# The value products of two cross attentions: f32 operands replaced by pairs of f16 halves

## The reference, cut to what matters

```python
# layer 1, x and ctx of width 256
Q, K, V = (q @ W_q.T), (ctx @ W_k.T), (ctx @ W_v.T)          # in 16 heads
scores = where(mask, einsum('bhqd,bhkd->bhqk', Q, K) / sqrt(16), -1e10)
x = x + (softmax(scores) @ V).reshape(B, 64, 256) @ W_proj.T + b_proj
# layer 3: q and k normalised to length 1, q times exp(scale), a bias instead of a mask
q, k = l2norm(x @ Wq + bq) * exp(min(scale_mul_log, log(100))), l2norm(ctx @ Wk)
x = x + (softmax(einsum('bhqd,bhkd->bhqk', q, k) + attn_bias) @ (ctx @ Wv)) @ Wo + bo
```

## Time and profile before

| | |
|---|---|
| median of 3 runs | 2602.82 us |
| the profiled execution | 2618.47 us, span 2616.8 us |
| mean granted TensorE clock | 0.959 |
| TensorE busy | 2341.9 us, 89% |
| VectorE, ScalarE, GpSimd busy | 64%, 48%, 32% |
| loop of layer 1, first to last value product | 409.3 to 785.6 us |
| loop of layer 3, first to last value product | 1949.7 to 2375.9 us |

### The profile page before, as it was taken

One profiled execution on the slowest core, in us unless ns is written; L12 is line 12 of the kernel. 1 busy time (PEld: TensorE's weight loads), 2 busy tenths in 40 slices (PEclk: granted clock), 3 DMA queues, 4 the chain that ended last, 5 costly groups with the idle time before them and its releaser, 6 DMA issues. The chain is left out here.

```text
span 2616.8 us, 44501 instructions
## 1 busy us (share of the span) xinstructions
PE 2341.9 (89%) x17350; PEld 1491.5 (57%) x17397; DVE 1665.0 (64%) x3199; ACT 1245.8 (48%) x2066; POOL 826.7 (32%) x669
## 2 busy tenths in 40 slices
PE   6866779999997879999999999699889999998898
PEld 4744446666673445566556666356546666666554
DVE  4986455545537666888888864644665565654577
ACT  2326234444454214555555554566445555554465
POOL 5610042224203421323333210045544444433153
PEclk8988899999998989999999999899989999999999
DMA  3200453322214016677767664033322222220132
GB/s 112 69 1 1 137 135 93 99 76 69 77 32 163 1 60 143 115 142 147 149 122 138 122 118 79 33 103 103 98 64 78 69 74 74 64 63 21 62 92 63
DMA packets 358467, 226.44 MB, mean 87 GB/s; under 512 B 289785, under 2 KB 326483, under 8 KB 358259
## 3 DMA queue, kind: packets, MB, share of 16 engines
q1 hardware_dynamic: 355186, 215.20, 34.0%
q0 software_dynamic: 3072, 8.39, 1.1%
HBM read 114.87 MB, written 0.52 MB: 44 GB/s over the span
## 5 line engine op out<-in xcount | busy, mean ns | idle before, releaser
L100 PE MATMUL PS<-hot 128*128 128x512 f16 x459 | 143.9, 456 | 90.0 <-DVE l0a_g L1087 17.5
L3875 POOL TENSOR_TENSOR l2x_rows<-l2x_rows,l2x_one 128x256 f16<-128x256 f32 (+2 forms) x95 | 100.2, 1081 | 379.5 <-DVE l2x_rows L1441 379.5
L3981 PE MATMUL PS<-l2x_rows,l2x_pth 128*128 128x512 f16 x832 | 200.3, 379 | 1.6 <-DVE l2x_mean L4178 1.6
L3625 DVE CUSTOM_DVE_ANT_0 l1x_junk<-PS,l1x_bias 128x1024 bf16<-128x1024 f32 (+1 forms) x128 | 123.2, 992 | 96.1 <-PE PS L3286 95.2
L3625 DVE CUSTOM_DVE_ANT_0 l3x_junk<-PS,l3x_bias 128x1024 bf16<-128x1024 f32 (+1 forms) x128 | 123.8, 991 | 46.6 <-PE PS L3286 45.5
L4171 DVE TENSOR_TENSOR l2x_pl<-l2x_sc,l2x_ph 128x1664 f16<-128x1664 f32 x64 | 123.8, 1934 | 39.8 <-ACT l2x_ph L4051 37.8
L4156 DVE CUSTOM_DVE_ANT_0 l2x_sc<-PS,l2x_bias 128x1665 f32<-128x1665 f32 x64 | 120.9, 1889 | 41.8 <-issue 40.6
L4069 ACT ACTIVATE l2x_meanT<-PS 128x256 f32<-128x256 f32 x64 | 24.6, 384 | 247.7 <-PE PS L3943 247.7
L3496 ACT ACTIVATE l3x_pT<-PS 128x512 f32<-128x512 f32 x144 | 84.6, 594 | 120.2 <-PE PS L3332 117.8
L100 PEld LDWEIGHTS PS<-hot 128*128 128x128 f16 x459 | 47.3, 112 | 165.7 <-issue 47.7
L3935 PE MATMUL PS<-l2x_kh,l2x_qth 128*128 128x512 f16 (+1 forms) x512 | 132.8, 341 | 3.6 <-DMA l2x_kl<-l2x_rows 3.6
(11 more groups left out here) (852 smaller groups left out, 6231.2 us busy)
## 6 DMA issues: line engine op xcount, KB each, us to landing
l2f_unit<-in_L_ffn_units_dram SPq DMA_DIRECT2D x36, 384.0 KB, 3.0
l3f_unit<-in_L_ffn_units_dram SPq DMA_DIRECT2D x34, 384.0 KB, 3.0
l1x_kst<-l1x_kh SPq DMA_DIRECT2D x128, 100.1 KB, 2.2
l3x_kst<-l3x_kh SPq DMA_DIRECT2D x128, 100.1 KB, 2.2
l2x_rows<-in_ctx_dram SPq DMA_DIRECT2D x8, 1536.0 KB
l1x_ctx<-in_ctx_t_dram SPq DMA_DIRECT2D x7, 1601.0 KB, 7.6
l3x_ctx<-in_ctx_t_dram SPq DMA_DIRECT2D x7, 1601.0 KB, 6.8
l1x_kst<-l1x_kl SPq DMA_DIRECT2D x64, 100.1 KB, 2.2
```

The source lines that it names most:

```text
L100: self.nc.tensor.matmul(self.PS[:, bank, :], self.hot[:, 0:P], self.hot[:], start=True, stop=True)
L3625: v.tensor_tensor_reduce(junk[:, slot(it), 0:n], slot_banks(it)[:, 0:n], bias[:, 0 if normed else b % 2, at:at + n], 1.0, LOWEST, ALU.add, ...
L3875: last = nc.gpsimd.tensor_tensor(high[:, at], of[:, at], one[0:p, at].unsqueeze(2).unsqueeze(3).to_broadcast([p, i, NC, P]), ALU.mult)
L3981: nc.tensor.matmul(PS[:, ACC, :], pth[:, u % 2, m, :], rows2[:, b % 2, :, :, m, :], start=(m == 0), stop=False)
```

## The change

The probabilities and the values are each held as two f16 halves, a high part and the rest. ScalarE computes each exponential twice, once into f16 (`ph`) and once into f32 (`p32`), both scaled by a constant factor; VectorE (for the tiles in `LOW_ON_VECTOR`) or GpSimd (the others) writes the difference into `pl`. `v33` holds 66 f16 columns for each pair: the 33 high ones and the 33 low ones; ScalarE writes the high ones, VectorE the low ones. A value product is then a matmul of all 66 columns with `ph` and a second of the 33 high columns with `pl`, both onto output partitions from 0, group `g` in bank `PV_BANK + g` for every batch entry. E adds the two halves in its matmul by `both_halves`. Item V's slot of PSUM is now given back by VectorE, after its own pass. In layer 3 only tiles 0 and 1 stay in `ON_VECTOR`. GpSimd's long passes are cut into pieces and put between its `low` passes. The core of the diff:

```diff
-    ON_VECTOR = list(range(4))
+    LOW_ON_VECTOR = (2, 3, 6, 7, 9, 11) if normed else (8, 10, 12)
+    KEY_SLOTS = {5: (0, 0), 7: (0, 1), 13: (1, 0), 15: (1, 1)}
+    CTX_SLOTS, CTX_PIECES = (17, 18, 19, 20, 21, 22, 23, 24) if normed else (14, 15, 17, 18, 20, 21, 23, 24), 8
+    WEIGHT_SLOTS = (2, 5, 8, 11, 14, 17)
+    ON_VECTOR = list(range(2 if normed else 4))
...
-        v33 = sb("v33", [P, 2, KT, R, VW])
+        v33 = sb("v33", [P, 2, KT, R, 2 * VW], F16)
...
+                def low(b, m, g):
...
+                    pool.wait_ge(exp_done, e + 1)
+                    nc.gpsimd.tensor_tensor(pl[0:n, (b * KT + m) % 2, g, :], p32[0:n, g, :], ph[0:n, (b * KT + m) % 2, g, :],
+                                            ALU.subtract).then_inc(low_pool, 1)
...
+                for i in range(CTX_PIECES):
+                    split_ctx(1, i)
+                for b in range(B):
+                    for x in range(STEPS):
+                        m, g = divmod(x, G2)
+                        if m not in LOW_ON_VECTOR:
+                            low(b, m, g)
...
+                        if b == B - 1 and later is not None and x in WEIGHT_SLOTS:
+                            later.split(pool, WEIGHT_SLOTS.index(x))
...
                     elif kind == "E":
                         pe.wait_ge(raw_copied, b + 1)
-                        for i in range(UG):
-                            last = nc.tensor.transpose(PS[:, bank, i * P:(i + 1) * P], raw[:, i * P:(i + 1) * P], k.ident[:])
+                        for u in range(R):
+                            last = nc.tensor.matmul(PS[:, bank, u * VW:(u + 1) * VW], raw[:, u // UG, u % UG * P:(u % UG + 1) * P],
+                                                    both_halves[:], start=True, stop=True)
...
                 def values(b, m, g):
-                    pe.wait_ge(exp_done, (b * KT + m) * G2 + g + 1)
+                    pe.wait_ge(low_by(m), low_count(b, m, g))
                     if g == 0:
-                        if m == 0 and b >= 2:
-                            pe.wait_ge(raw_copied, b - 1)
-                        pe.wait_ge(v_read, b * NV + m // VT + 1)
+                        if m == 0 and b >= 1:
+                            pe.wait_ge(raw_copied, b)
+                        pe.wait_ge(v_low, b * NV + m // VT + 1)
                     for i in range(UG):
                         u = g * UG + i
-                        at = (u % 2) * S
-                        last = nc.tensor.matmul(PS[at:at + VW, PV_BANK + b % 2, (u // 2) * P:(u // 2 + 1) * P],
-                                                v33[0:n, b % 2, m, u, :], pT[0:n, (b * KT + m) % 2, g, i * P:(i + 1) * P],
-                                                start=(m == 0 and u < 2), stop=(m == KT - 1), skip_group_check=True)
+                        at = slice(i * P, (i + 1) * P)
+                        nc.tensor.matmul(PS[0:2 * VW, PV_BANK + g, at], v33[0:n, b % 2, m, u, :], ph[0:n, (b * KT + m) % 2, g, at],
+                                         start=(m == 0 and i == 0), stop=False, skip_group_check=True)
+                        last = nc.tensor.matmul(PS[0:VW, PV_BANK + g, at], v33[0:n, b % 2, m, u, 0:VW], pl[0:n, (b * KT + m) % 2, g, at],
+                                                start=False, stop=(m == KT - 1), skip_group_check=True)
...
-                        nc.scalar.activation(raw[:], PS[:, PV_BANK + b % 2, :], ACT.Copy).then_inc(raw_copied, 1)
+                        nc.scalar.activation(raw[:], PS[0:2 * VW, PV_BANK:PV_BANK + G2, :], ACT.Copy).then_inc(raw_copied, 1)
...
-                    nc.scalar.activation(to, of, ACT.Exp, scale=1.0 / S_SCALE).then_inc(exp_done, 1)
+                    nc.scalar.activation(ph[0:n, (b * KT + m) % 2, g, :], of, ACT.Exp, bias=p_ln[0:n, :], scale=1.0 / S_SCALE)
+                    nc.scalar.activation(p32[0:n, g, :], of, ACT.Exp, bias=p_ln[0:n, :], scale=1.0 / S_SCALE).then_inc(exp_done, 1)
...
+                    elif kind == "V":
+                        dve.wait_ge(v_high, b * NV + c + 1)
...
+                        for y in range(x.start, x.stop):
+                            last = v.scalar_tensor_tensor(
+                                v33[0:part, b % 2, y, :, VW:VW + F],
...
+                                V_ONE / SW, v33[0:part, b % 2, y, :, 0:F], ALU.mult, ALU.subtract)
+                        last.then_inc(v_low, 1)
+                        dve.wait_ge(v_low, b * NV + c + 1)
+                        v.memset(ticks[:, slot(it):slot(it) + 1], 0.0).then_inc(read[slot(it)], 1)
```

More of the change, by code:

```diff
@@ L2924, in context_attention, with low_count @@
     ONE_HOT = 2.0 ** 6 if normed else 1.0
-    ON_VECTOR = list(range(4))
+    ON_VECTOR = list(range(2 if normed else 4))
     def vector_count(b, m, g):
         return G2 * (b * len(ON_VECTOR) + sum(1 for x in ON_VECTOR if x < m)) + (g if m in ON_VECTOR else 0)
+    def low_count(b, m, g):
+        mine = [x for x in range(KT) if (x in LOW_ON_VECTOR) == (m in LOW_ON_VECTOR)]
+        return G2 * (b * len(mine) + mine.index(m)) + g + 1
     def pieces(at, n):
@@ L3176, in make_bias, with split_keys @@
                     pool.wait_ge(bias_made, b + 1)
-                def split_keys(b):
-                    if b == 0:
+                def split_keys(b, c, h):
+                    if b == c == h == 0:
                         pool.wait_ge(const_rows, 16)
-                    for c in range(NC):
[L3182 to L3192, removed]
@@ L3194, in _ @@
-                if normed:
-                    split_keys(0)
+                    at, n = halves[h]
+                    pool.wait_ge(unit_keys, (b * NC + c) * NH + h + 1)
+                    if h == 0 and b > 0:
+                        for u in range(c * RC, (c + 1) * RC):
+                            pool.wait_ge(stacked[u], b * STACK)
+                    hold()
+                    for _, x, i in pieces(at, n):
+                        last = nc.gpsimd.tensor_tensor(kh[:, c, x:x + i], k32[:, x:x + i], one[:, 0:1].to_broadcast([P, i]), ALU.mult)
@@ new lines, in split_keys, with split_ctx @@
+                    link(last)
+                    for _, x, i in pieces(at, n):
+                        last = nc.gpsimd.tensor_tensor(kl[:, c, x:x + i], k32[:, x:x + i], kh[:, c, x:x + i], ALU.subtract)
+                    last.then_inc(key_low, 1)
+                    pool.wait_ge(key_low, (b * NC + c) * NH + h + 1)
+                def split_ctx(b, i):
+                    if i == 0:
+                        pool.wait_ge(ctx_loaded, b * 16)
+                        pool.wait_ge(made, number[(LAST_USE, b - 1)] + 1)
+                        hold()
+                    c, h = divmod(i // 2, 2)
+                    at, n = ((0, 801), (801, 800))[h]
+                    high, wide = ctxh[:, c, at:at + n], ctx32[:, c, at:at + n]
+                    if i % 2 == 0:
+                        link(nc.gpsimd.tensor_tensor(high, wide, one[:, 0:1].to_broadcast([P, n]), ALU.mult))
+                    else:
+                        last = nc.gpsimd.tensor_tensor(ctxl[:, c, at:at + n], wide, high, ALU.subtract)
+                    if i == CTX_PIECES - 1:
+                        last.then_inc(ctx_parts, 1)
+                        pool.wait_ge(ctx_parts, FIRST_CTX + b)
@@ L3200, in _ @@
                 nc.gpsimd.tensor_tensor(k.X[:], k.X[:], b_o[:].unsqueeze(1).to_broadcast([P, NT, D]), ALU.add).then_inc(x_ready, 1)
[L3202 to L3216, removed]
+                for i in range(CTX_PIECES):
[5 more added lines that the diff above has]
+                            low(b, m, g)
+                        if b + 1 < B and x == 0 and not normed:
+                            make_bias(b + 1)
+                        if b + 1 < B and x in KEY_SLOTS and normed:
+                            split_keys(b + 1, *KEY_SLOTS[x])
+                        if b + 2 < B and x in CTX_SLOTS:
+                            split_ctx(b + 2, CTX_SLOTS.index(x))
+                        if b == B - 1 and later is not None and x in WEIGHT_SLOTS:
+                            later.split(pool, WEIGHT_SLOTS.index(x))
             @block.tensor
@@ L3672, in _ @@
                                 item(it)
+                            b_, x = divmod((b * KT + m) * G2 + g - 1, STEPS)
+                            if x // G2 in LOW_ON_VECTOR and b_ >= 0:
+                                low(b_, x // G2, x % G2)
+                if KT - 1 in LOW_ON_VECTOR:
+                    low(B - 1, KT - 1, G2 - 1)
                 for it in tail:
```

85 lines of the change are left out of this document (58 added, 27 removed).

## The result

The changed kernel takes 3132.53 us (median of 4 runs, 3125.27 to 3141.15), the kernel before 2601.07 in the runs beside it (2598.28 to 2603.06): ratio 1.204, interval 1.201 to 1.207. The forecast was 2963, the range 2875 to 3060. The direction was right, the amount too small: 531 us more and not 360.

The account below looks back on a forecast made before the run. The prediction took TensorE to bound the loops and summed 327 + 21 + 7 + 9 + 4 + 2 - 10 = +360 us onto 2602.8, giving 2963 us. The range was 2875 to 3060.

Parts of the forecast that it names:

- What bounds the kernel: In both layers' loops TensorE is the limit, busy 89% of the span, so its extra time is the loop's.
- The value product: In both loops a tile's value matmuls go from 1.10 to 2.67 us; over 208 tiles +327 us.
- E: Per batch entry, four transposes become eight f32 matmuls of 33 columns: +1.35 us for each of 16, +21 us.
- the price of a change: On TensorE, each switch between wide and narrow stationary costs 0.093 us, plus 0.025 or 0.012 for the load.
- C: TensorE's clock falls: Rival: 1.2 GHz for a tenth to a fifth of the two loops, +70 to +140 us, 3060 us; chance 0.12.
- The waits: In the two loops TensorE's waits for slots get shorter under longer value products: -10 us, bounds 0 and -25.
- Ahead of the loops: VectorE gets 13 passes of 0.484 us before the loops, partly in idle time: +9 us (0 to 14).
- at the layers' ends: One exponential, one `low` and the wider R stand in the bare chain from scores to output: +4 us.
- The cover: In the loops the other engines' added work and waits hide under TensorE; otherwise a few us per batch entry.
- rival A: In value products, shape changes cost nothing when alternating one by one: about 2600 us, not slower; chance 0.06.
- Rival D: A wait for GpSimd's or ScalarE's chain stands bare in most batch entries, 3 us in 16: 3010 us; chance 0.12.

Follow-up runs that it names:

- the kernel without `low`: Changed kernel with 66-column second value products, without the passes making the probabilities' low half (second product reuses the high half): ratio 1.037 to the kernel before.
- the 66-column kernel: Changed kernel whose second value product also takes all 66 columns, so no change of shape stands inside a tile: ratio 1.077 to the kernel before.

## Why the prediction was wrong

**What bounds the kernel:** right. The loops are TensorE's before and after; the profile's growth outside them is 21 us.

**The value product:** right to a hundredth of a microsecond, 2.67 us for a tile, and with it E and the price of a change read from two places of the old trace. The medians of a tile show that it holds at 4, 8 and 16 changes, and the median of the changed kernel's tiles is 2.665 us. The Trainium skill (TensorEngine Tiling (Array Packing), Key Properties) says that a change of tiling mode drains TensorE; the traces fit that, with some 0.09 us lost at each change.

**The step that failed is the clock.** "C: TensorE's clock falls" was priced at +70 to +140 us and given 0.12; the sum carried nothing for it. Measured are +135 us, at the upper end. The price was right part by part: the loops stood at 1.2 GHz for 366 us, which is 231 us at the full clock, a fifth of the loops' 1200, with 0.6 of it streamed, as C assumed at its upper end. The chance was not, and the range ended at 3060, inside C's own 3033 to 3103. What was on the page already: the new product streams 0.88 of its 2.67 us, twice as long in spacing as in work, and there is a stretch, the last batch entry, in which nothing but such products and short score groups is left. I looked at the mean over the loops and weighed the case as one chance for all, where the last entries needed a term of their own (about 20 us each: 68.4 and 70.2 us measured, of which some 45 and 47 are work at 2.4 GHz and 4 and 3 waits). That would have been some 40 of the 135; the other 95 came in the seven entries ahead, in many shorter stretches, and what sets each of them off is open. "TensorE busy" misled: this is the stretch before the fall and the one after it, in the kernel after.

```profile
957.40:971.10 13.70, 13.70 (x103) 8.54 (x101) 7.07 (x14) 8.06 (x15) 2.30 (x2) 1.00 0.00 1
971.10:1043.00 71.90, 70.16 (x343) 41.21 (x346) 9.59 (x16) 32.73 (x53) 23.05 (x20) 0.50 0.00 1
```

TensorE is busy for all of 13.70 us, and then the clock falls to 1.2 GHz and stays there to the loop's end. A matmul's bar in the trace is 0.22 us long while it streams for 0.055; at a start each 0.167 us the bars touch. The Trainium skill says it (Perfetto Trace Analysis, Identifying the Most-Contended Engine): the busy share of matmuls is not a good measure of how close TensorE is to its limit. The trace agrees, with 100% beside 0.88 us of streaming in 2.67.

**The waits** went the other way: +25 us, not -10. In layer 1 the slot that VectorE now releases costs 25.3 us; ScalarE's release cost 3.3 us there, and the largest wait in that loop was a key product's for another slot, 8.5. The prediction counted VectorE's passes as busy time and didn't follow what stands behind V's release on TensorE. Ahead of the loops it was 13 us for 9, at the layers' ends 8 for 4.

**The cover** ("if that cover were gone ... a few us for each batch entry") was priced too low, though it doesn't show in the change's own time. With the losses of shape removed, the chain of `exp`, `exp`, `low` and the orders around it leave the kernel 202 us slower than before, and its waits are 7 us longer in each batch entry than the changed kernel's. Of the 202 us, 107 go with `low`. The other 95 are, in the kernel without `low`, 67 us of longer waits, 18 of clock, 21 outside the loops, and about 10 less of TensorE's own work; which part of those waits is the second exponential's, beside V's slot (25.3 us in layer 1), wasn't told apart. By the 66-column kernel, rival A would have come out at a ratio near 1.08 and not at 2600 us. Rival D, a bare wait for GpSimd's chain, was right about the mechanism and wrong about the kernel: it shows only in the variants with quicker products.

## What to carry to other kernels

Where a change makes TensorE's stream thin, read streaming per distance between starts for each stretch, not the busy share, and give a stretch that holds nothing else a term for the clock in the sum. Count changes between wide and narrow stationary operands as instructions of their own, and group what has one shape. A chain that is covered by the bottleneck is priced by taking the bottleneck's loss away, tile by tile, before it is called free.

## What the runs showed of the hardware

- A change between 66 and 33 columns costs some 0.11 us with the load behind it, equally at 4, 8 and 16 changes in a tile (1.321, 1.768 and 2.665 us for a tile, 0.894 without); it isn't cheaper when shapes alternate one by one.
- Two f16 products of 33 columns on output partitions 0 and 64 run side by side as f32 ones do: eight start and clear in 0.34 us, with the change at the end in it, where eight of f32 take 0.99, the same change in it.
- A TensorE that was busy for 13.70 of 13.70 us, streaming 0.88 us of each 2.67 in the value products, lost its clock, and work whose result is overwritten can shorten a stretch: 11 us more of 512-column matmuls made it 13 us shorter (68.4 to 55.0), the same in layer 3 made it 9 us shorter (70.2 to 61.0).
